# A second SBUF buffer for the transposed FFN weights of a two-layer kernel on eight cores

## What is computed

```python
def fp4_linear(x, w):
    xq = fp4_quant_dequant(x)
    wq = fp4_quant_dequant(w)
    return jnp.einsum('bsk,nk->bsn', xq, wq)
gate = fp4_linear(x, w_gate)          # w_gate, w_up: 2816 x 1024
y = fp4_linear(x, w_up)
h = jax.nn.silu(gate) * y
return fp4_linear(h, w_down)
```

## Time and profile before

| | us |
|---|---|
| two timed runs | 6354.53 and 6490.58 |
| their median | 6422.55 |
| the profiled execution | 6280.04 |
| its span (core 3, the slowest) | 6278.7 |
| spans of the 8 cores | 6254.9 to 6278.7 |
| PE busy | 3512.8 (56%) |
| DVE busy | 2093.6 (33%) |
| ACT busy | 1252.0 (20%) |
| POOL busy | 650.1 (10%) |

### The profile page before, as it was taken

How to read it: one execution, slowest core, us unless ns; L and a number is a source line. 1 busy time by engine, 2 the same in 40 slices (tenths; PEclk the granted TensorE clock), 3 DMA queues, 4 the chain that set the end, 5 groups by cost and what they waited for, 6 DMA issues and landing times.

```text
span 6278.7 us, 45778 instructions; the slowest of 8 cores (6254.9 to 6278.7 us)
## 1 busy us (share of the span) xinstructions
PE 3512.8 (56%) x15560; PEld 1490.7 (24%) x15560; DVE 2093.6 (33%) x3269; ACT 1252.0 (20%) x2020; POOL 650.1 (10%) x435
## 2 busy tenths in 40 slices
PE   1933234344302656500904664288988989889890
PEld 0400010100101333300401221133433434334340
DVE  2154444521255666755232113221212111112122
ACT  1222223233211222100132110321111212112121
POOL 0022222200022322322000000000000000000000
PEclk9955555555555878755957887589999999999995
DMA  4011111100000000001442113503032030230304
GB/s 98 1 34 44 37 42 37 52 10 7 31 27 27 14 27 14 13 32 39 147 111 44 17 14 130 139 1 54 1 54 49 5 54 5 50 54 1 54 1 157
DMA packets 114258, 271.18 MB, mean 43 GB/s; under 512 B 41040, under 2 KB 41552, under 8 KB 113008
## 3 DMA queue, kind: packets, MB, share of 16 engines
q0 software_dynamic: 72576, 119.34, 10.3%
q1 hardware_dynamic: 41456, 148.91, 7.0%
HBM read 299.33 MB, written 53.48 MB: 56 GB/s over the span
## 4 chain that ended last, share of the span: by engine, by line
PE 49%; DVE 18%; DMA 10%; ACT 9%; issue 5%; POOL 5%; DVEq 3%; another core or an unknown queue 0%; SPq 0%; ACTq 0%; POOLq 0%
PE pq L1542 14%; PE pq L1568 14%; PE pq L1211 4%; DMA d_b2r<-b_row 3%; PE pq L427 2%; ACT a_expA L400 2%; PE pq L385 2%; ACT a_expB L401 2%; PE pq L279 2%; POOL b_q L553 2%; PE pq L429 2%; PE pq L868 1%; POOL b_hb L556 1%; DMA d_s1t<-s 1%; DVE b_q L534 1%
## 5 line engine op out<-in xcount | busy, mean ns | idle before, releaser
L1542 PE MATMUL pq<-d_tT,d_w1e 128*128 128x512 bf16 x4096 | 908.3, 384 | 35.1 <-ACT d_hTh L1550 35.1
L1568 PE MATMUL pq<-d_w2e,d_hTh 128*128 128x512 bf16 x4096 | 889.2, 379 | 33.4 <-ACT d_hTh L1550 33.4
L1584 DVE SCALAR_TENSOR_TENSOR d_acc<-pq,d_comb,d_acc 128x512 f32<-128x512 f32 x256 | 192.3, 751 | 1620.4 <-PE pq L1568 1620.4
L427 PE MATMUL pq<-a_expA,a_vsb 128*65 128x512 bf16 x320 | 194.3, 607 | 746.6 <-DVE a_expB L412 462.0
L1550 ACT ACTIVATE d_hTh<-pq,d_b1s 128x512 bf16<-128x512 f32 x512 | 351.5, 687 | 1236.5 <-PE pq L1542 1236.5
L1542 PEld LDWEIGHTS pq<-d_tT,d_w1e 128*128 128x128 bf16 x4096 | 404.5, 99 | 537.7 <-issue 67.5
L1568 PEld LDWEIGHTS pq<-d_w2e,d_hTh 128*128 128x128 bf16 x4096 | 398.5, 98 | 524.1 <-issue 48.3
L400 ACT ACTIVATE a_expA<-pq 128x512 bf16<-128x512 f32 x320 | 190.9, 596 | 891.2 <-PE pq L389 891.2
L1211 PE MATMUL pq<-c_xn2T,c_wsl 128*128 128x512 bf16 x1024 | 263.8, 404 | 162.2 <-ACT c_ga L1221 81.6
L409 DVE TENSOR_TENSOR a_expA<-a_expA,a_masks_s 128x512 bf16<-128x512 bf16 x128 | 62.3, 486 | 611.6 <-ACT a_expB L401 611.3
L553 POOL TENSOR_TENSOR b_q<-b_q,b_blk 128x1024 f32<-128x1024 f32 (+2 forms) x96 | 160.8, 1675 | 937.8 <-DVE b_q L547 874.8
(11 more groups left out here) (213 smaller groups left out, 4032.0 us busy)
## 6 DMA issues: line engine op xcount, KB each, us to landing
d_w1e<-w1T POOLq DMA_DIRECT2D x8, 4096.0 KB, 26.2
d_w2e<-w2T POOLq DMA_DIRECT2D x8, 4096.0 KB, 27.1
a_wrowA<-wgu POOLq DMA_DIRECT2D x44, 512.0 KB, 4.7
b_xt<-x SPq DMA_DIRECT2D x32, 512.0 KB, 4.6
wq_pre<-a_qbfA POOLq DMA_DIRECT2D x44, 256.0 KB, 2.6
b_qbf<-wq_pre SPq DMA_DIRECT2D x22, 512.0 KB, 3.9
b_wdr<-wd SPq DMA_DIRECT2D x8, 1408.0 KB, 6.5
a_xt<-x SPq DMA_DIRECT2D x16, 512.0 KB, 3.6
```

The lines of the kernel that those rows point to most:

```text
L427: p.te.matmul(pq[4][0:65, :], vA, expA[:, esl * 512:(esl + 1) * 512], start=(kc == 0), stop=(kc == nkc - 1))
L1542: inst = p.te.matmul(bank[:], w1e[:, j * MOE_H + hc * 128: j * MOE_H + (hc + 1) * 128], tT[:, j * S + hf * 512: j * S + (hf + 1) * 512], s ...
L1568: inst = p.te.matmul(bank[:], hTh[:, j * 512 + tr * 128: j * 512 + (tr + 1) * 128], w2e[:, j * D + dh * 512: j * D + (dh + 1) * 512], star ...
```

## The change

A second buffer `qbfB` of the same size as `qbf` (4 KB per partition) is allocated. Groups alternate between the two, counted by `pj`. SP's wait before a load is for the end of the transposes of group `pj - 2`, kept in `te_wtr_hist`, in place of group `pj - 1`; group 0 keeps its three waits and group 1 has none of its own. The transposes read from the group's buffer. Nothing else differs: the same loads, transposes and copies are issued in the same order on each engine. The branch without `wq_pre` isn't used here.

```diff
+    qbfB = nc.alloc_sbuf_tensor("qbfB", [128, 2 * D], BF16)
...
+        te_wtr_hist = {}
...
-                        if wk == 0:
+                        pj = wk // 2
+                        qb_ = [qbf, qbfB][pj % 2]
+                        if pj == 0:
                             p.sy.wait_ge(p.gw1.h, p.gw1.v)
                             p.sy.wait_ge(p.gw2.h, p.gw2.v)
                             p.sy.wait_ge(p.ted.h, te_tr[-1])
-                        else:
-                            p.sy.wait_ge(p.ted.h, te_wtr_prev)
-                        sp_ = [p.sw2, p.sw3][(wk // 2) % 2]
+                        elif pj >= 2:
+                            p.sy.wait_ge(p.ted.h, te_wtr_hist[pj - 2])
+                        sp_ = [p.sw2, p.sw3][pj % 2]
                         p.sy.dma_start(
-                            out=qbf[:].rearrange("p (c d) -> p c d", c=2),
+                            out=qb_[:].rearrange("p (c d) -> p c d", c=2),
...
-                                qbf[:, c * D + j * 128: c * D + (j + 1) * 128],
+                                qb_[:, c * D + j * 128: c * D + (j + 1) * 128],
                                 ident[:])
                     inst.then_inc(p.ted.h, 1)
                     te_wtr_prev = p.ted.bump()
+                    te_wtr_hist[wk // 2 - 1] = te_wtr_prev
```

More of the change, by code:

```diff
@@ L806, in narrative @@
                     else:
+                        qb_ = qbf
                         for c in range(2):
```

## The result

| | kernel before | changed kernel |
|---|---|---|
| median | 6329.6 us (36 runs) | 6285.4 us (38 runs) |
| ratio | | 0.9933, 95% interval 0.991 to 0.9956 |
| profiled execution, slowest span | 6278.7 us | 6242.7 us |
| spans of the 8 cores | 6254.9 to 6278.7 us | 6216.0 to 6242.7 us |
| gate/up stage, mean of 8 cores | 673.8 us (671.1 to 675.9) | 639.2 us (637.8 to 640.6) |

Many runs of both kernels are lengthened by a lower clock on some cores; the runs within 0.3% of the fastest of each kernel have medians of 6279.0 us (11 runs) and 6245.8 us (16 runs), 33.2 us apart. The change gains 0.5 to 0.7%: less than the 2% that would be called faster.

What follows compares the result with a forecast made beforehand. No engine bounds the whole kernel; in gate/up preparation, TensorE's 71.1 us of waits for weight loads set the pace. From 6280.0 us, 30.8 and 3.0 off and 0.8 added gave 6247.0 us, range 6220 to 6400.

Steps and rivals of the forecast that it cites:

- The 16 waits and what lies under them: Gate/up weight preparation: 67.4 us of load waits go, 16 PSUM evacuation waits of 2.29 us (36.6 us) appear; gain 30.8 us.
- The cover of the loads: Third and fourth weight groups of each slice: loads finish with about 2 us to spare under the evacuation waits.
- First slice: Start of gate/up: two loads issued back to back delay the first group by 0 to 1.6 us, taken as +0.8.
- B at full clock: Second weight group of the five later slices: transposes fit in the full-clock stretch, worth 0 to 3.3 us, taken as 3.0.
- Sum: Whole kernel, worked out on core 3: 6280.0 - 30.8 - 3.0 + 0.8 = 6247.0 us, 0.53% less.
- The other cores: They waited 64 to 71 us for the load, so gain 3 to 7 us less, without overtaking core 3.
- Passed on: After each preparation: PE still arrives after POOL's quantization, each slice shifts as a whole, and the shift reaches the kernel's end.
- The full clock during C and D: Rival, chance 0.05: PE stays at full clock through the whole weight preparation, 19.7 us more gained, 6227 us.
- Late loads: Rival, chance 0.06: third and fourth groups wait again, loads usable only over 6.4 us after issue; at 8.4 us, 6267.
- Hidden anyway: Rival, chance 0.04: the gain is given back at a later wait all cores meet, such as large weight loads; 6280.
- Slower by writing beside the transposes: Rival, chance 0.03: loads writing the neighbouring SBUF buffer stretch the 16 groups; at 2.5 us each, 6287 us.

Runs made afterwards that it cites:

- second profile of the changed kernel: The changed kernel, unaltered, timed and profiled once more in a later comparison with the kernel before: ratio 0.9939, interval 0.9893 to 0.9984.

## Why the prediction was right

*The 16 waits and what lies under them.* Forecast for core 3: 67.4 us of load waits go, 36.6 us of evacuation waits appear, 30.8 gained. There 34.9 us appeared, 32.5 gained. The 2.29 us that I had taken from the gate matmul were 0.11 too long for a transpose. That the waits appear where PSUM was still single, and that they are real, is shown by the run with two bank pairs (20.8 us less) and the run with the same pairs and one buffer (nothing).

*The cover of the loads.* Forecast: about 2 us. C started 5.3 us after its load's issue, not 6.4, since B was short, and D 6.2 us after its own; and one extra load of the same size, 1.7 us by what it added before, brought 5 of core 3's groups to the edge and cost the stage 0.6 us. The term was right, and barely: four buffers gained nothing, a load a little longer than the extra one would have begun to cost. One step under it was wrong: only one load was to be in flight at a time. With B short, D's load is issued 3.2 us behind C's and so at times before C's has landed; over the stage 4 to 12 loads of a core, the first slice's pair apart, met the tail of the one before, for up to 1.2 us. No group waited for it.

*First slice.* Forecast: A late by 0 to 1.6 us, taken as 0.8. The wait was 3.83 us before and 4.08 changed on the mean of the cores, 0.25 more: 0 to 0.3 on seven cores and 1.2 on one. In the second profile of the changed kernel it was 3.81 to 4.05, 3.91 on the mean. So it lay near the lower bound, as by the Trainium skill's rule of ring order ("DMA: Bandwidth & Descriptors", Queues, rings and completion order); what held up the one core is not shown.

*B at full clock.* Forecast: 1.22 us in place of 1.87, 3.0 us in all. Measured 1.05 in 39 of 40 cases, 0.82 us each, 4.1 on core 3. I had taken the pace of transposes of line 761 in their eight, 0.61 us, whose own end weighs more in 8 than in 16. It hung by a thread, as the sum of starts had shown: B ends at 2083.0 on core 3, and the clock had fallen by 2083.3.

*Sum.* 32.5 + 4.1 = 36.6 us for core 3, against 34.8 of its stage: 1.8 us were given back in the product halves. In the second slice it is 96.34 us before and 96.97 changed from the first gate matmul to the next A, at the head of which the clock climbs (gate matmul to first SiLU 5.4 us, not 5.1). I had not forecast this. Forecast total 33.0; measured 33.2 between the medians of the runs near the fastest, 34.6 by the stage.

*The other cores, and luck.* The prediction gave them 3 to 7 us less than core 3, since most waited less for the loads. Core 5 did gain 4.3 us less (30.5); the six others gained 33.9 to 38.2, against 34.8 on core 3. The step that fails is that a slice shifts as a whole by what its preparation saves. On all cores but core 3 the product halves became shorter, by 1.8 to 5.3 us in sum. The times from one slice's A to the next show how even this is. For the second to fifth slices they were 119.1 to 119.6 us before, on every core, though the preparations in them took 20.9 to 23.1; changed, 112.4 to 112.8, but for the one slice in which B missed the full clock by 0.8 us, 115.6. A slice's length thus did not follow its waits one for one. In the mean of the cores the preparations gave 32.2 us and the product halves 2.3. Worked out on core 1, with 63.9 us of load waits, the same sum would have forecast 7 us less (26), and core 1 gained 34.5. That the forecast met the whole so closely is in part luck: on core 3 the evacuation waits cost 1.7 us less than forecast, B gave 1.1 more, the first load cost 0.7 less, and the product halves took 1.8 back.

*Passed on.* The head of a slice never waited for POOL, as forecast, and the stages behind shifted whole: the mean span fell by 34.3 us, the mean stage by 34.6.

*The time itself.* 6247.0 was forecast on the footing of the profiled execution, which gave 6244.2 us; the median of 38 runs, 6285.4, lies 38 us above, inside the range that I had drawn up to 6400 from two runs of the kernel before. A range of 180 us says little about a gain of 33. Those two were not typical: over 36 runs its median was 6329.6, not 6422.6.

*The rivals.* The full clock during C and D did not come: 0.50 in the third row above, so for bursts 2.2 us apart attention was the right model. The Trainium skill's section on HAM oscillation ("TensorE: Matmul & The Clock Gate"), read as a promise that closing load waits keeps the clock up, would have misled by 20 us. Late loads: only with an extra load per group. Two loads of core 2 did take over 5 us (5.2 and 5.6), which I had named as a sign of being wrong, and none but the first group waited. Hidden anyway: the mean span shows that it was not. Slower by writing beside the transposes: D's transposes took 1.87 us as ever while the DMA engines moved 291 GB/s in their first microsecond, and B took 1.05 while a load moved 309 GB/s.

## What to carry to other kernels

A second buffer is worth the wait it removes less the wait that lies under it; look in the same trace for an instruction that waits for only that second thing, and take its idle time as what will remain. That gives the gain of the stretch in which the waits lie; what follows it can take up or give back some (here 1.8 us given back on one core, 1.8 to 5.3 gained on the seven others), so check the sum on more cores than one. Buffers count along the whole path: SBUF alone gained 34.6 us here, PSUM alone 0.3, both 55.4, and with two more SBUF buffers 65.4 (four cores). Judge an edit of half a per cent by the length of its own stage over all cores, not by the span of the slowest.

## What was not expected of the hardware

The granted clock that rises behind a slice's opening 24 transposes, and is down again before C, can be used: work that is brought into that stretch ran in 1.05 us, not 1.87. Whether it rises depended on more than the length of the run: 39 of 40 openings of later slices, 1 of 4 where the same length was made up in the first slice (of the four cores at a mean granted clock of 0.84 to 0.85 in the stage). And PE busy in bursts of 1.87 us, 2.18 apart, did not hold or raise it.

From the second to the fifth slice, the time from A to the next A was the same on all cores to within half a microsecond, before and changed, though before their preparations differed by up to 2.1 us; and the one B that was 0.8 us slower went with a slice 3.1 longer (core 5). The clock's steps are the likely link, since the clock climbs at the head of each product half, but no run here shows it alone.
